# Attention of a graph transformer layer: score and product steps issued in pairs instead of one by one

## The reference, cut to what matters

```python
q = (x @ Wq.T + bq) * HD ** -0.5; k = x @ Wk.T + bk; v = x @ Wv.T + bv     # per head 1250 x 64
logits = einsum('bthd,bshd->bhts', q, k)          # temporal expert: -inf above the diagonal
att = softmax(logits, axis=-1)
o = einsum('bhts,bshd->bthd', att, v)
```

## Time and profile before

| | |
|---|---|
| runs | 2074.18, 2077.14, 2081.05 us (median 2077.14) |
| the profiled execution | 2076.11 us, of it a span of 2074.3 us |
| granted TensorE clock, mean | 0.957 |
| busy: PE, DVE, ACT, POOL | 1881.6, 1181.2, 719.4, 330.3 us |
| attention, from the first to the last product | 555.6 to 1767 us of the span |

### The profile page before, as it was taken

How to read it: one execution, slowest core, us unless ns; L and a number is a source line. 1 busy time by engine, 2 the same in 40 slices (tenths; PEclk the granted TensorE clock), 3 DMA queues, 4 the chain that set the end, 5 groups by cost and what they waited for, 6 DMA issues and landing times.

```text
span 2074.3 us, 31417 instructions
## 1 busy us (share of the span) xinstructions
PE 1881.6 (91%) x10647; PEld 1676.6 (81%) x10647; DVE 1181.2 (57%) x2374; ACT 719.4 (35%) x1363; POOL 330.3 (16%) x336
## 2 busy tenths in 40 slices
PE   1899999965899999999999999899999999877998
PEld 0688567754799999989889898789999989676886
DVE  6677567767465555564746646655556555632332
ACT  0223201003454444445545444245544544210110
POOL 3210001002101202020100003100000013455340
PEclk9999999975899999999999999989999999988999
DMA  3101001013200100020000000000000002012111
GB/s 102 31 6 42 11 11 31 1 39 121 86 11 16 42 21 11 1 85 37 13 9 11 11 1 16 21 11 11 6 11 6 6 1 76 31 33 69 41 31 50
DMA packets 24394, 60.59 MB, mean 29 GB/s; under 512 B 2522, under 2 KB 4790, under 8 KB 23373
## 3 DMA queue, kind: packets, MB, share of 16 engines
q1 hardware_dynamic: 24260, 58.74, 8.7%
HBM read 44.87 MB, written 13.86 MB: 28 GB/s over the span
## 4 chain that ended last, share of the span: by engine, by line
PE 80%; DVE 10%; POOL 2%; issue 2%; DMA 1%; ACT 1%; SPq 1%; DVEq 1%; POOLq 0%; ACTq 0%
PE ps L2174 20%; PE ps L2060 12%; PE ps L2229 7%; PE ps L2156 5%; PE ps L2160 5%; PE ps L1874 5%; PE ps L2117 5%; PE ps L1954 4%; PE ps L2258 3%; PE ps L1986 3%; DVE max_part L1649 3%; PE ps L2138 2%; DVE share L1666 2%; PE ps L1887 1%; PE ps L2185 1%
## 5 line engine op out<-in xcount | busy, mean ns | idle before, releaser
L2174 PE MATMUL ps<-p_raw,v_ones 125*128 125x250 f32 x2080 | 535.0, 379 | 4.2 <-DVE feat L1668 3.2
L1649 DVE TENSOR_REDUCE max_part<-ps 125x2 f32<-125x500 f32 x520 | 329.9, 674 | 285.9 <-PE ps L2117 269.3
L1243 ACT ACTIVATE p_raw<-ps 125x500 f32<-125x500 f32 x520 | 305.0, 587 | 365.2 <-PE ps L2160 361.5
L2174 PEld LDWEIGHTS ps<-p_raw,v_ones 125*128 125x128 f32 x2080 | 362.1, 191 | 33.7 <-issue 4.0
L1666 DVE RECIPROCAL share<-ps 64x250 f32<-64x250 f32 x120 | 206.7, 1722 | 64.7 <-PE ps L2174 61.9
L2156 PE MATMUL ps<-q_both_a,k_both_a 128*125 128x250 f32 x520 | 184.5, 375 | 1.8 <-ACT q_row_b L1216 1.8
L2156 PE MATMUL ps<-q_both_b,k_both_b 128*125 128x250 f32 x520 | 181.9, 371 | 0.0
L878 POOL CAST w_hi<-w_raw 128x512 fp32r<-128x512 f32 x44 | 29.0, 660 | 897.0 <-issue 396.0
L1500 DVE TENSOR_SCALAR onehot<-iota_h,win_key,key_t 125x320 f16 x453 | 169.1, 373 | 0.5 <-issue 0.4
L1499 DVE TENSOR_SCALAR onehot<-iota_h,low_t 125x125 f16 x453 | 127.2, 281 | 59.4 <-PE ps L1986 30.7
L2060 PE MATMUL ps<-xa_hi,w_hi 128*128 128x418 f32 (+1 forms) x448 | 152.0, 339 | 8.9 <-DVE xb_lo L1418 4.1
(11 more groups left out here) (365 smaller groups left out, 3466.7 us busy)
## 6 DMA issues: line engine op xcount, KB each, us to landing
w_raw<-in_w_mlp SPq DMA_DIRECT2D x32, 256.0 KB, 2.6
w_raw<-in_w_gps SPq DMA_DIRECT2D x16, 256.0 KB, 2.6
w_raw<-in_w_tp SPq DMA_DIRECT2D x16, 256.0 KB, 2.6
w_raw<-in_w_sp SPq DMA_DIRECT2D x12, 256.0 KB, 2.7
w_raw<-in_w_cr SPq DMA_DIRECT2D x12, 256.0 KB, 2.6
d_xt<-xb_hi SPq DMA_DIRECT2D x1, 2508.0 KB, 9.3
d_xt<-xb_lo SPq DMA_DIRECT2D x1, 2508.0 KB, 14.9
xa_hi<-d_xt SPq DMA_DIRECT2D x1, 2508.0 KB, 9.6
```

Source lines behind the costliest of these rows:

```text
L1243: act.activation(p_raw[:, g % PR, :], ps[0:TOK, g % 2, 0:4 * TOK], ACT.Exp, scale=SCALE).then_inc(s_exp, 1)
L1649: dve.tensor_reduce(part[:, y, :, j], ps[0:TOK, bank, 0:4 * TOK].rearrange("p (h k) -> p h k", h=2), AX.X, ALU.max)\
L2174: ins = pe.matmul(ps[:, bank, 0:2 * TOK], v_ones[:, kt, h, :], p_raw[:, g % PR, cols], start=(b == 0 and x == 0), stop=last)
```

## The change

Steps go two at a time. TensorE's list becomes: score steps g+2 and g+3, the side tasks of g, product steps g and g+1, for even g. `LEAD` is 2, `p_raw` has four buffers (`PR`) and the query slots are four (`QR`). The planner visits even steps only, with double credit and up to six tasks (of them up to four M) in a visit; within a visit T and R stand last. Due dates are moved ahead by 3 to 4 steps. ScalarE does `exponent(g+2)`, the second halves of the tasks of g-2, `exponent(g+3)`, the first halves of the tasks of g. VectorE does the low parts of the tasks of g-2, the maxima of g, then `unit_out` for g-2 and g-1.

```diff
-QR = 3
-LEAD = 1
-PR = 3
+QR = 4
+LEAD = 2
+PR = 4
...
-        credit = min(credit + 1.05 * sum(near) / (FIRST[n + 1, 0] - g), 2.4)
+        if g % 2:
+            continue
+        credit = min(credit + 2.1 * sum(near) / (FIRST[n + 1, 0] - g), 3.2)
...
-                if task[0] in LINEAR and g < linear_at + 2 or used.count(task[0]) >= (2 if task[0] == "M" else 1):
+                if task[0] in LINEAR and g < linear_at + 2 or used.count(task[0]) >= (4 if task[0] == "M" else 1):
...
-            if found is None or len(used) == 3:
+            if found is None or len(used) == 6:
...
-        side[g].sort(key=lambda task: task[0] == "T")
+        side[g].sort(key=lambda task: task[0] in "RT")
...
-        for g in range(first, end):
+        for g in range(first, end, 2):
             if g + LEAD < end:
-                steps.append(("S", g + LEAD))
-            steps += SIDE[g] + [("P", g)]
+                steps += [("S", g + LEAD), ("S", g + LEAD + 1)]
+            steps += SIDE[g] + [("P", g), ("P", g + 1)]
...
-                for g in range(first, end):
+                for g in range(first, end, 2):
                     if g > first:
-                        for task in SIDE[g - 1]:
+                        for task in SIDE[g - 2]:
                             last_out(task)
                     for what, *at in SIDE[g]:
                         if what == "M":
                             maximum(*at)
-                    if g > first and ends(g - 1):
-                        unit_out(g - 1)
+                    for x in (g - 2, g - 1):
+                        if g > first and ends(x):
+                            unit_out(x)
```

More of the change, by code:

```diff
@@ L183, in due_dates @@
             gf, tasks = FIRST[n, i], maxima(n, i)
-            due["R", n, i] = gf - 4
+            due["R", n, i] = gf - 7
             for x, task in enumerate(tasks):
-                due[task] = gf - 5 - 2 * (len(tasks) - 1 - x) // 3
-            due["Q", n, i] = gf - 8 - 2 * len(tasks) // 3
+                due[task] = gf - 9 - 2 * (len(tasks) - 1 - x) // 3
+            due["Q", n, i] = gf - 12 - 2 * len(tasks) // 3
         gf, start = FIRST[n, 0], due["Q", n, 0]
@@ L190, in due_dates @@
             due["K", n, p] = start - 1 - 4 * (2 - p)
-            due["V", n, p] = gf - 6 - 3 * (2 - p)
+            due["V", n, p] = gf - 8 - 3 * (2 - p)
         for _, _, h, b in value_turns(n):
-            due["T", n, h, b] = first_use(n, h, b) - 2
+            due["T", n, h, b] = first_use(n, h, b) - 4
     for x in range(FB + 1):
@@ L212, in allowed @@
         x = 5 * n + rest[0]
[L213 removed]
+        free = LAST[(x - QR) // 5, (x - QR) % 5] - 1 if x >= QR else 0
         return max(free, later(("K", n, 2), 2), later(("Q", (x - 1) // 5, (x - 1) % 5), 2))
@@ L222, in allowed @@
         before = order[:order.index(task)][-1:]
-        return max([later(("V", n, 2), 2), last_use(n - 1, h, b) + 1] + [later(x, 0) for x in before])
+        return max([later(("V", n, 2), 2), last_use(n - 1, h, b) + 2] + [later(x, 0) for x in before])
     return max(FIRST[1, 2] + 4, later(("F", n - 1), 3) if n else 0)
@@ L273, in plan_steps @@
         if task[0] == "R":
-            assert g <= FIRST[task[1], task[2]] - LEAD - 1, task
+            assert g < FIRST[task[1], task[2]] // 2 * 2 - LEAD, task
     return side, at
@@ L377, in bank_plan @@
             use = [2 + unit_of(entry[1]) % 2] if STEP[entry[1]][3] == 0 else []
-            slot = entry[1] + 1
+            slot = entry[1] // 2 + 1
         elif kind == "J":
@@ L1307, in _ @@
                     if g > first:
-                        for task in SIDE[g - 1]:
+                        for task in SIDE[g - 2]:
                             second_out(task)
+                    if g + LEAD < end:
+                        exponent(g + LEAD + 1)
                     for task in SIDE[g]:
                         first_out(task)
-                for task in SIDE[end - 1]:
+                for task in SIDE[end - 2]:
                     second_out(task)
@@ L1740, in _ @@
                             maximum(*at)
-                    if g > first and ends(g - 1):
-                        unit_out(g - 1)
-                for task in SIDE[end - 1]:
+                    for x in (g - 2, g - 1):
+                        if g > first and ends(x):
+                            unit_out(x)
+                for task in SIDE[end - 2]:
                     last_out(task)
-                unit_out(end - 1)
+                for x in (end - 2, end - 1):
+                    if ends(x):
+                        unit_out(x)
             for p in range(3):
```

## The result

The changed kernel takes **2093.39 us** (median of 4 runs, 2092.0 to 2094.8) against 2078.93 (4 runs, 2074.18 to 2081.05): ratio 1.0073 [1.0052, 1.0093], slower. The forecast was 2092. The profiled execution of after is 2094.8 us, its span 2093.0 at a mean clock of 0.954 (before 2074.3 and 0.957). Of all executions behind this text two stand far outside the others of their kernel, one of before (4726.5 us) and one of e10 (3178.9 us); neither is used in a ratio.

The account below looks back on a forecast made before the run. TensorE was taken to bound the kernel, busy 91% of the span. Waits gone -31, waits remaining +3, banks +21, VectorE late +10, short units +13 make +16 on 2076.1: 2092 us, own range 2084 to 2102, whole range 2060 to 2112.

Parts of the forecast that it names:

- What goes, with what stays of it: TensorE's waits in R, M, T and P: 31 us gone, but +3 for M and R places that still wait.
- Banks and lateness: Side tasks wait for their pair's first maximum's bank in 81 pairs, +21; VectorE running late in 21 of them, +10.
- Short units: First products of causal passes 4 to 7 wait for divisions now placed behind their pair's maxima: +13 us.
- Openings and all outside attention: The two openings and everything outside attention were taken as unchanged: 0 us.
- Causal passes no shorter: Among the signs of being right: the causal stretch of attention would be no shorter than before.
- A change of kind costs nothing: TensorE going from product to score matmuls has no price, so 260 fewer such changes save 0 us.
- Rival (d): Each change from product to score on TensorE costs 0.18 us, so 47 us are saved: 2045 us; chance 0.06.
- Rival (a): Bank waits do not come about, the first M's reduce being finished when the fifth task arrives: 2061 us; chance 0.14.
- (b): Bank waits are there but VectorE's lateness is not, and short units cost half: 2076 to 2081 us; chance 0.14.
- (c): VectorE becomes the pace in bursts, lateness spreading to all 81 places, 2131 us, or half, 2112; chance 0.12.
- second and third terms: Bank waits with VectorE's lateness (+21 and +10), and short units at causal pass starts (+13), added as separate costs.

Follow-up runs that it names:

- e10: Changed kernel with at most three maxima per pair, two ahead of the projection and one behind, and VectorE's divisions ahead of the maxima: 2048.49 us.
- e4: Changed kernel with score and product steps alternating again inside each pair, ScalarE's list matched to it: 2089.75 us.
- e1: Changed kernel with, in pairs holding a projection, two maxima ahead of the projection and the others behind it: 2089.39 us.
- e9: Changed kernel with the projection between two and two maxima, and VectorE's divisions also between the first two maxima and the others: 2082.08 us.
- e7: Original kernel, steps one by one, with VectorE's division of the previous step's unit ahead of the step's maxima: 2083.07 us.

## Why the prediction was right

The time came out within 2 us of the forecast, and by its mechanism: the waits named as going went, and those named as coming came, in nearly the places that were counted. That the sum is so close is in part luck. Its three measured terms below make -28 + 25 + 12.5, or +10 instead of +16, and what it had at nothing, some 7 to 9 us of the profiled execution's 18.7, made up for that. By its own steps, with sizes by starts:

- **What goes, with what stays of it (-31 + 3 = -28).** R 12.7 and T 5.8 gone, M behind its queries 9.7 to 5.6, products behind an M or a mask 5.4 as known from before: 28.0. Right.
- **Banks and lateness (+21 + 10 = +31).** Measured 22.6 - 2.1 in the bank places and 18.6 - 14.0 in the projections behind them: +25, in 74 places instead of 81. A place without lateness costs 0.35 us (forecast 0.31: the reduces of this burst start 0.6 apart, less than the 0.65 of the earlier trace rows, but the stalled matmul gives up 0.11 more behind its own start). Lateness was the smaller part, over-sized by about a half: of the 22.6, 6.9 lie above 0.24 a place. M to M grew by about 1 us beside it, which the forecast had at nothing.
- **Short units (+13).** T to product 3.9 (three of 1.26), product to product 3 x 0.89 and 1.66, and 4.3 once behind a mask in pass 7: 12.5. Right, place by place: 2.1 a pass in passes 4 to 6, where 2.3 to 2.5 were forecast, and 6.0 in pass 7 against 5.8.
- **Openings and all outside attention (0).** Wrong, by +4 in the profiled execution: the first product comes 2.0 us later (557.6 for 555.6). From the opening's R to it there are 12.3 us instead of 9.4, since two more score steps and two more M stand in between, most of them at half the clock (the two rows below, PEclk 0.83 and 0.77); R itself comes 0.9 earlier. And from the last product to the end there are 309.9 us instead of 307.9, which is less than the scatter of runs and not settled.

```profile
535.00:555.60 20.60, 16.50 (x99) 15.72 (x99) 7.46 (x13) 8.18 (x19) 1.88 (x2) 0.83 0.06 14
535.00:557.50 22.50, 18.41 (x105) 17.56 (x104) 8.14 (x15) 8.62 (x20) 1.87 (x2) 0.77 0.04 12
```

- **The clock (0, not named).** Matmuls at half the clock cost attention 2 to 3 us more than before (37.5 us of it instead of 30.7).
- **Causal passes no shorter.** Wrong in part: passes 4, 5 and 6 are 1.5, 2.0 and 3.0 us shorter than before, for T's and R's waits stood there; pass 7, which also holds the opening of the cross attention, is 3.7 longer, and there the clock alone costs 3 to 4 us more (31 us at half of it instead of 22). The terms were right as sums over attention, not stretch by stretch.
- **A change of kind costs nothing.** Right, and shown by e4. Rival (d) falls, and with it the reading of the Trainium skill ("TensorE: Matmul & The Clock Gate", on single matmul latency) by which 260 changes would be worth 42 us.
- **Rival (a)**, banks free in time, falls: 74 places. **(b)**, lateness absent, is where the forecast was nearest to failing; 7 us of it, not 10. **(c)** falls in after, but VectorE's order did set the time of e1 and e9. Its price for half of the places, 2112, should read 2106: 24 us of lateness instead of 10 is 14 more than 2092.

What the prediction did not see is that its second and third terms are not independent. It added them, and after's time bears the sum out; yet taking away one of them is worth 4 us or none, not its 25 or 12, since in a list that is strict on both engines the next tight place takes over (and in e1 some 5 us went to the clock). Both together are worth 35.

Pass 0 is 3 to 11 us longer in all the kernels in pairs than in before (104.5 us there, 113.0 in after, 109.6 in e10). That is in part no loss: the planner puts 144 projection matmuls into it in after and 156 in e10, where before has 120, and pass 11 is 6.4 us shorter in after. Of after's 8.5 us some 3 are such work moved ahead and 5.6 are waits; in e10 it is 5 of work and no more waiting than before.

What stays open is why the kernels differ in how long TensorE is granted half the clock. It is worth up to 5 us in the comparisons above, and differences smaller than that are not shown to be the edit's own.

## What to carry to other kernels

Making the units of an order larger buys distance between a result and its reader, and spends it on distance between a buffer's write and its reuse: count both, and cap the burst at one less than the banks (here three maxima for four banks) before giving up the idea. In a strict list put the work whose input is already there first and that which waits for the other engine behind it, and see that nothing tight stands behind a long one in the middle. When a cure for a real wait brings nothing, apply the cure of the next wait together with it before judging either. Both rules need the room that a larger block gives: in single steps the division first made R wait 9 us more (e7).

## What the hardware showed that I had not expected

- A stall of TensorE by about 0.35 us leaves no idle time in the view of waits, as the modelled end of the matmul ahead covers 0.28 and the stalled one's record begins 0.11 early (0.30 to the next instead of 0.19 at 700.60). Of about 25 us of bank waits that view showed 7.1 under PE; the other 52 places appear only under the weight loads, PEld, with 20.8 us of their idle time.
- TensorE's busy time grew by 16.6 us for the same 10647 matmuls (1881.6 to 1898.2) where the span grew by 18.7: a busy share of 91% before and after hides nearly all of the loss.
- T, four transposes on 64 partitions, costs on entering and on leaving: 0.28 us from the last matmul of a projection to it, where 0.19 is usual, and 0.199 from its last record to a product (median of 50), where 0.11 is usual. Some 0.09 each way. After, PE:

```profile
1097.29 0.35 PE L2067 MATMUL ps<-xa_hi,w_lo 128*128 128x418 f32 x1
1097.57 0.65 PE L2145 MATMUL ps<-ident,feat 64*125 64x64 f32 x4
```
